# A graph layer with residual and normalisation: VectorE selects the edges of a group four groups ahead throughout, not six

## The chip, the cores and the metric

The kernel runs on one core of a Trainium2 chip. The time is device time in microseconds (us). Engines are called TensorE (PE in the rows, PEld for its weight loads), VectorE (DVE), ScalarE (ACT), GpSimd (POOL) and SyncE (SP).

## What is computed

`x` has 100,000 nodes of 128 features, and there are 50,000 edges (`src`, `dst`) sorted by `dst`. Cut to what matters:

```python
messages = jnp.einsum('ei,oi->eo', x[col], W) + b
out = jax.ops.segment_sum(messages * agg_weight, row, num_segments=x.shape[0])
x = _layernorm(x + out, axis=-1)        # row = src, col = dst
```

So each node receives the projected feature rows of the nodes at the other end of its edges, plus the bias once per edge; that sum is added to the node's own row, and every row is normalised.

## The kernel before

**Two stages.** In the first 270 us or so the 50,000 edges are sorted by receiving node into lists of at most 128 edges; the result is `table`, which holds for each place in a list the row of `x` to gather and the node that receives it. The change doesn't touch that. The second stage walks over 196 groups of 512 nodes (g = 0 to 195; GA is 196). It is written as one stream of instructions for each engine, tied by semaphores that count.

**Lists and periods.** Eight groups make a period (SPAN_G = 8) and have 17 lists. A list belongs to the group in which its window of nodes starts: within a period the groups own 3, 2, 2, 3, 2, 2, 2 and 1 lists. `u` is the group's number modulo 8. The last nodes of a period also fall into the first list of the next period.

**One group, engine by engine.**

- GpSimd gathers the rows of each list into `xg` (L527, 17 gathers a period). It may start on group g once TensorE has summed group g - 8.
- VectorE's `select(g)` splits each gathered fp32 value into three bf16 parts (L984 writes `rest`, L989 writes `xl`) and makes a 0/1 matrix `sel` for each list of the group (L986). It waits for the gathers and for `s_agg`.
- TensorE's `aggregate(g)` multiplies the three parts with `sel` and adds them in PSUM (L707, L709, L711); behind an odd group stand the counts of edges (L721).
- ScalarE's `keep_sums(g)` copies the sum to SBUF as `aggT` (L1094).
- TensorE's `project(g)` multiplies `aggT` with the weights (L737), and adds the bias for an even group and its neighbour (L734).
- VectorE's `add_x(g)` waits for `project(g)` (`s_out`) and adds the loaded `x` (L995, writes `h`); `moments(g)` takes the statistics (L1002); for a pair of groups `invert` and `recentre` follow (L1008, L1013).
- ScalarE's `spread_of` takes the root (L1102), and `normalise` writes `y` in four instructions (L1109). SyncE loads `xt` and stores `y`.

**Order on TensorE.** Round r holds `aggregate(r)` and then `project(r - 2)`: A(6), P(4), A(7), P(5), A(8), P(6) and so on. A(g) is used below for the sums of group g, P(g) for its projection and S(g) for `select(g)`.

**What the sums of a group wait for.** A(g) needs S(g). The last group of a period needs more, since it also uses the first list of the next period. This is the line, in `aggregate`:

```python
pe.wait_ge(s_lower, min(g + 2, GA) if u % SPAN_G == SPAN_G - 1 else g + 1)
```

`s_lower` counts the finished selects, so for u = 7 the sums of group g wait until S(g + 1) is done.

**Order on VectorE.** It is the loop that the change touches. An iteration g holds `add_x(g)`, the selects that `lead` asks for, `moments(g)`, and after every odd group `invert` and `recentre` for the pair. `lead(g)` is how many groups the selects run ahead: 4 for groups 0 to 3, 5 for groups 4 to 7, and 6 from group 8 on. Iteration 3 and iteration 7 therefore hold two selects, and from then on iteration g holds S(g + 6). The buffers `sel`, `rest` and `xl` hold one period (XR = 1), `xg` holds two (RX = 2).

Of the kernel before, what the change touches and what calls it, by code (L numbers as in the profile page):

```python
# [16 lines left out]
def gnn_resnorm_kernel(nc, x, src, dst, W, b, agg_weight, hi_scratch, place_scratch, out, most=128):  # L17
# [56 lines left out]
    with ctx:  # L74
# [6 lines left out]
        def at_least(eng, s, count):  # L81

            if not isinstance(count, int) or count > 0:
                eng.wait_ge(s, count)
# [256 lines left out]
        def rounds(stages):  # L341

            for i in range(GA + max(lag for _, lag in stages)):
                for stage, lag in stages:
                    g = i - lag
                    if 0 <= g < GA:
                        stage(g, g % R, g // R, g // SPAN_G, g // SPAN_G % RX, g // SPAN_G // RX)
# [396 lines left out]
        def _(dve):  # L744
# [163 lines left out]
            def decode(lo, hi):  # L908
                c = slice(lo, hi)
                after(V.tensor_tensor(i2[:, c], i2[:, c], other2[:, c], OR))  # L910
                V.tensor_scalar(emp[:, c], i1[:, c], FULL, FULL, XOR, AND)
                V.tensor_scalar(low4[:, c], i2[:, c], 15 << 25, 25, AND, LSR)
                after(V.tensor_scalar(tabi[:, c], i1[:, c], 8191 << 16, 12, AND, LSR))
                after(V.tensor_tensor(low4[:, c], low4[:, c], tabi[:, c], OR))
                after(V.tensor_scalar(tabi[:, c], emp[:, c], 30, None, LSR))
                after(V.scalar_tensor_tensor(table[:, c, 0], tabi[:, c], part[:], low4[:, c], ALU.mult, ALU.add))
                after(V.tensor_scalar(emp[:, c], emp[:, c], 20, None, LSR))
                after(V.tensor_scalar(tabq[:, c], i2[:, c], (GN - 1) << 16, 16, AND, LSR))
                return V.tensor_tensor(table[:, c, 1], tabq[:, c], emp[:, c], OR)
# [52 lines left out]
            with dve.Else():  # L972
                decode(head, NB).then_inc(s_idx, 1)

                def select(g, u, n, period, m, mn):
                    if g == 0 or g == RX * SPAN_G:
                        dve.wait_ge(s_idx, 1 + period // RX)
                    at_least(dve, s_agg, g - (XR * SPAN_G - 2))
                    mine = [k for k in CLASS[u % SPAN_G] if period * LISTS + k < NB]
                    lists = slice(mine[0], mine[-1] + 1)  # L980
                    if u % SPAN_G == 0:
                        dve.wait_ge(s_first[m], 16 * mn + 16)
                    dve.wait_ge(s_rest[m][u % SPAN_G], 16 * mn * len([k for k in CLASS[u % SPAN_G] if k]) + 16 * len([k for k in mine if k]))
                    V.tensor_tensor(rest[:, m % XR, lists], xg[:, m, lists], top[:, m, lists, :, 1], ALU.subtract).then_inc(s_upper, 1)  # L984
                    for k in mine:
                        V.tensor_scalar(sel[:, m % XR, k, 0:WIDTH[k]], iota_win[:, WIN[k]:WIN[k] + WIDTH[k]],  # L986
                                        table[:, period * LISTS + k, 1:2], None, ALU.is_equal).then_inc(s_sel, 1)
                    dve.wait_ge(s_upper, g + 1)
                    V.tensor_tensor(xl[:, m % XR, lists], rest[:, m % XR, lists], middle[:, m % XR, lists, :, 1], ALU.subtract).then_inc(s_lower, 1)  # L989

                def add_x(g, u, n, period, m, mn):
                    dve.wait_ge(s_out, g + 1)
                    dve.wait_ge(s_x[u], 16 * n + 16)
                    at_least(dve, s_y, 4 * g - 4 * R + 4)
                    V.tensor_tensor(h[:, u].rearrange("p j d -> p (j d)"), OUT[u % RO][:],  # L995
                                    xt[:, u].rearrange("p j d -> p (j d)"), ALU.add).then_inc(s_h, 1)

                def moments(g, u, n, period, m, mn):

                    dve.wait_ge(s_h, g + 1)  # L1000
                    for j in range(0, 4, 2):
                        V.bn_stats(stats[:, u, j:j + 2].rearrange("p two f -> p (two f)"),  # L1002
                                   h[:, u, j:j + 2].rearrange("p two d -> p d two")).then_inc(s_stats, 1)

                def invert(g, u, n, period, m, mn):
                    if u % 2:
                        dve.wait_ge(s_std, g // 2 + 1)
                        V.reciprocal(rstd[:, u - 1:u + 1], std[:, u - 1:u + 1]).then_inc(s_rstd, 1)  # L1008

                def recentre(g, u, n, period, m, mn):  # L1010
                    if u % 2:
                        dve.wait_ge(s_rstd, g // 2 * 2 + 1)
                        V.scalar_tensor_tensor(shift[:, u - 1:u + 1], stats[:, u - 1:u + 1, :, 1], -1.0, rstd[:, u - 1:u + 1],  # L1013
                                               ALU.mult, ALU.mult).then_inc(s_rstd, 1)

                def one(stage, g):
                    if 0 <= g < GA:
                        stage(g, g % R, g // R, g // SPAN_G, g // SPAN_G % RX, g // SPAN_G // RX)

                lead = lambda g: min(6, 4 + g // 4)  # L1020
                for g in range(lead(0)):
                    one(select, g)
                for g in range(GA + 1):
                    one(add_x, g)
                    for ahead in range(g + lead(g), g + 1 + lead(g + 1)):
                        one(select, ahead)
                    one(moments, g)
                    one(invert, g - 1)
                    one(recentre, g - 1)
# [107 lines left out]
```

## Time and profile before

| | us |
|---|---|
| median of 3 runs | 838.07 |
| lowest, highest | 833.6, 838.79 |
| span of the profiled execution | 834.4 |

The span is that of one execution, from its first to its last instruction, and lies inside the range of the three runs. The page does not give time outside the span.

| engine | busy us | share |
|---|---|---|
| VectorE | 769.2 | 92% |
| TensorE matmul | 756.2 | 91% |
| ScalarE | 660.2 | 79% |
| GpSimd | 494.7 | 59% |

These are shares of the whole span. The second stage begins at about 270 us, and from 340 to 800 us it runs evenly; the views of that stretch say more than the page's average. "PEclk" is the TensorE clock granted: 1.00 is 2.4 GHz, 0.5 would be 1.2 GHz.

### The profile page before, as it was taken

What the parts mean: (1) busy time and instruction counts of PE and PEld (TensorE: products, weight loads), DVE (VectorE), ACT (ScalarE), POOL (GpSimd) and SP (SyncE); (2) the same over time, 40 slices, a digit from 0 to 9 for tenths busy, and PEclk for the clock granted to TensorE, in tenths of its full rate; (3) what the DMA queues carried; (4) which work ended last, traced back from release to release, by engine and by line L of the source; (5) the groups of instructions that cost most, each with busy time, mean ns of one, the idle gap of its engine ahead of it and who ended that gap; (6) DMA issues with size and microseconds to landing.
All of it is one profiled execution on the core that took longest, in us unless ns stands there. A gap on an engine that the chain in (4) does not pass through costs nothing.

```text
span 834.4 us, 23648 instructions
## 1 busy us (share of the span) xinstructions
PE 756.2 (91%) x8073; PEld 550.6 (66%) x8073; DVE 769.2 (92%) x2547; ACT 660.2 (79%) x1659; POOL 494.7 (59%) x510
## 2 busy tenths in 40 slices
PE   4889999999999978999998899999999999899894
PEld 3844555555554656777777777777777777677773
DVE  7989999999998788999999999998999999999995
ACT  2157878787885368899888889888889888888898
POOL 2024333333421777777777777777777777777750
PEclk9999999999999999999999999999999999999998
DMA  2001110111113257888777788777777878778773
GB/s 78 2 27 40 28 40 28 32 36 28 41 35 103 61 177 223 246 243 254 235 253 232 238 241 247 246 237 235 233 248 245 254 234 248 228 251 252 232 240 135
DMA packets 78148, 139.46 MB, mean 167 GB/s; under 512 B 16864, under 2 KB 17900, under 8 KB 78028
## 3 DMA queue, kind: packets, MB, share of 16 engines
q1 hardware_dynamic: 62476, 110.50, 39.5%
q0 software_dynamic: 15552, 27.43, 14.4%
q8 instruction: 66, 1.08, 0.5%
q14 instruction: 54, 0.44, 0.2%
HBM read 86.04 MB, written 51.83 MB: 165 GB/s over the span
## 4 chain that ended last, share of the span: by engine, by line
PE 37%; DVE 27%; issue 13%; DMA 8%; POOL 7%; ACT 7%; ACTq 0%; POOLq 0%; SPq 0%; DVEq 0%
PE bank L737 10%; DMA xg<-in_x,table 8%; POOL xg L527 7%; PE bank L660 5%; DVE stats L1002 4%; DVE oh_s L891 4%; DVE sel L986 3%; ACT y L1109 3%; PE bank L707 3%; PE bank L711 3%; PE bank L709 3%; DVE oh_t L893 3%; DVE rest L984 3%; DVE xl L989 2%; PE bank L553 2%
## 5 line engine op out<-in xcount | busy, mean ns | idle before, releaser
L527 POOL DMA_INDIRECT xg<-in_x,table x417 | 415.7, 997 | 147.5 <-issue 100.3
L1109 ACT ACTIVATE y<-h,shift,rstd 128x128 f32<-128x128 f32 x784 | 321.6, 482 | 24.5 <-DVE shift L1013 24.4
L737 PE MATMUL bank<-wT,aggT 128*128 128x128 f32 x1568 | 229.0, 290 | 0.0
L737 PEld LDWEIGHTS bank<-wT,aggT 128*128 128x128 f32 x1568 | 191.6, 193 | 27.4 <-issue 10.8
L709 PE MATMUL bank<-sel,rest 128*128 128x385 bf16 (+25 forms) x708 | 183.7, 261 | 0.0
L707 PE MATMUL bank<-sel,xg 128*128 128x385 bf16 (+25 forms) x708 | 176.6, 262 | 3.2 <-DVE xl L989 3.0
L711 PE MATMUL bank<-sel,xl 128*128 128x385 bf16 (+25 forms) x708 | 174.9, 261 | 0.0
L479 POOL DMA_INDIRECT place_scratch<-word_col,place_row x69 | 71.6, 1038 | 131.3 <-DVE place_row L882 108.0
L1002 DVE BATCH_NORM_STATS2 stats<-h 128x6 f32<-128x256 f32 x392 | 148.0, 418 | 0.2
L995 DVE TENSOR_TENSOR h<-bank,xt 128x512 f32<-128x512 f32 x196 | 133.7, 682 | 5.9 <-PE bank L737 5.1
L660 PE MATMUL bank<-oh_t,oh_s 128*128 128x417 bf16 x644 | 129.0, 345 | 6.2 <-ACT oh_s L1073 0.8
L1094 ACT COPY aggT<-bank 128x512 f32<-128x512 f32 x196 | 110.8, 565 | 20.2 <-PE bank L711 20.1
L986 DVE TENSOR_SCALAR sel<-iota_win,table 128x385 bf16<-128x385 f16 (+1 forms) x417 | 121.0, 336 | 0.0
L891 DVE TENSOR_SCALAR oh_s<-iota_nb,slot,word_col 128x128 bf16<-128x128 f16 x322 | 107.3, 333 | 0.6 <-PE bank L660 0.4
L984 DVE TENSOR_TENSOR rest<-xg 128x384 f32<-128x384 f32 (+1 forms) x196 | 85.1, 434 | 23.5 <-DMA xg<-in_x,table 22.8
L893 DVE TENSOR_SCALAR oh_t<-iota_nb,t_now 128x417 bf16<-128x417 f16 x322 | 106.0, 329 | 0.0
L1073 ACT ACTIVATE oh_s<-oh_s,ratio_col 128x128 bf16<-128x128 bf16 x322 | 102.8, 393 | 3.3 <-DVE oh_s L891 2.2
L660 PEld LDWEIGHTS bank<-oh_t,oh_s 128*128 128x128 bf16 x644 | 58.0, 98 | 57.3 <-DVE oh_t L893 14.1
L989 DVE TENSOR_TENSOR xl<-rest 128x384 bf16<-128x384 f32 (+1 forms) x196 | 84.5, 431 | 0.0
L707 PEld LDWEIGHTS bank<-sel,xg 128*128 128x128 bf16 x708 | 69.8, 99 | 19.7 <-DVE xl L989 3.4
L709 PEld LDWEIGHTS bank<-sel,rest 128*128 128x128 bf16 x708 | 69.0, 98 | 18.0 <-issue 0.5
L711 PEld LDWEIGHTS bank<-sel,xl 128*128 128x128 bf16 x708 | 69.0, 98 | 16.0 <-issue 0.5
(156 smaller groups left out, 743.1 us busy)
## 6 DMA issues: line engine op xcount, KB each, us to landing
xt<-in_x SPq DMA_DIRECT2D x195, 256.0 KB
out<-y SPq DMA_DIRECT2D x195, 256.0 KB
xg<-in_x,table POOLq DMA_INDIRECT x417
hi_row<-hi_scratch SPq DMA_DIRECT2D x50, 128.0 KB
place_scratch<-word_col,place_row POOLq DMA_INDIRECT x69
place_scratch<-scattered SPq DMA_DIRECT2D x1, 417.0 KB, 3.5
scattered<-place_scratch SPq DMA_DIRECT2D x1, 417.0 KB, 3.2
src_rows<-in_src SPq DMA_DIRECT2D x1, 192.0 KB
```

Source lines behind the costliest of these rows:

```text
L527: nc.gpsimd.indirect_dma_start(out=xg[:, m, k], out_offset=None, in_=x, in_offset=bass.IndirectOffsetOnAxis(ap=table[:, period * LISTS + k ...
L660: last = nc.tensor.matmul(TABLES[w][:, 0:NB], hot, oh_t[:, no % RING], start=(no == 0), stop=False, skip_group_check=True)
L707: nc.tensor.matmul(AGG[q][:, nodes], top[:, ring, k, :, 1], sel[:, half, k, cols], start=(i == 0), stop=False, skip_group_check=True)
L709: nc.tensor.matmul(AGG[q][:, nodes], middle[:, half, k, :, 1], sel[:, half, k, cols], start=False, stop=False, skip_group_check=True)
L711: last = nc.tensor.matmul(AGG[q][:, nodes], xl[:, half, k], sel[:, half, k, cols], start=False, stop=(i == len(lists) - 1), skip_group_che ...
L737: last = nc.tensor.matmul(OUT[u % RO][:, nodes[j]], aggT[:, u % RO, nodes[j]], wT[:], start=False, stop=True, skip_group_check=True)
L891: V.tensor_scalar(oh_s1[:, no % RING], iota_nb[:, 0:P], slot[:, q, i:i + 1], w1_col[:, k * BC + i:k * BC + i + 1], ALU.is_equal, ALU.mult) ...
L893: V.tensor_scalar(oh_t[:, no % RING], iota_nb[:], t_now[:, q, i:i + 1], None, ALU.is_equal).then_inc(s_oh, 1)
L986: V.tensor_scalar(sel[:, m % XR, k, 0:WIDTH[k]], iota_win[:, WIN[k]:WIN[k] + WIDTH[k]], table[:, period * LISTS + k, 1:2], None, ALU.is_eq ...
L995: V.tensor_tensor(h[:, u].rearrange("p j d -> p (j d)"), OUT[u % RO][:], xt[:, u].rearrange("p j d -> p (j d)"), ALU.add).then_inc(s_h, 1)
L1002: V.bn_stats(stats[:, u, j:j + 2].rearrange("p two f -> p (two f)"), h[:, u, j:j + 2].rearrange("p two d -> p d two")).then_inc(s_stats, 1)
L1109: nc.scalar.activation(y[:, u, j], h[:, u, j], ACT.Identity, bias=shift[:, u, j:j + 1], scale=rstd[:, u, j:j + 1]).then_inc(s_y, 1)
```

## The change

```diff
-                lead = lambda g: min(6, 4 + g // 4)
+                lead = lambda g: 4
                 for g in range(lead(0)):
                     one(select, g)
                 for g in range(GA + 1):
```

Every iteration g now holds S(g + 4) and nothing else of the selects. No instruction is added or removed, and no other engine's order changes.

The first place is VectorE's order around the first select of a period, in the evenly running part. The row with `s_first0` is the start of that select, S(8k), and `s_x2` marks `add_x` of a group with u = 2, `s_x4` one with u = 4. Before:

```order
L995 TENSOR_TENSOR h<-bank6,xt 128x512 [waits s_y,s_x2,s_out]
L984 TENSOR_TENSOR rest<-xg 128x384 [waits s_rest0_0,s_first0,s_agg]
L986 TENSOR_SCALAR sel<-iota_win,table 128x385 x3
L989 TENSOR_TENSOR xl<-rest 128x384 [waits s_upper]
L1002 BN_STATS stats<-h 128x6 [waits s_h]
L1002 BN_STATS stats<-h 128x6
L1008 RECIPROCAL rstd<-std 128x8 [waits s_std]
L1013 SCALAR_TENSOR_TENSOR shift<-stats,rstd 128x8 [waits s_rstd]
L995 TENSOR_TENSOR h<-bank7,xt 128x512 [waits s_y,s_x3,s_out]
```

After:

```order
L995 TENSOR_TENSOR h<-bank2,xt 128x512 [waits s_y,s_x4,s_out]
L984 TENSOR_TENSOR rest<-xg 128x384 [waits s_rest0_0,s_first0,s_agg]
L986 TENSOR_SCALAR sel<-iota_win,table 128x385 x3
L989 TENSOR_TENSOR xl<-rest 128x384 [waits s_upper]
L1002 BN_STATS stats<-h 128x6 [waits s_h]
L1002 BN_STATS stats<-h 128x6
L1008 RECIPROCAL rstd<-std 128x8 [waits s_std]
L1013 SCALAR_TENSOR_TENSOR shift<-stats,rstd 128x8 [waits s_rstd]
L995 TENSOR_TENSOR h<-bank3,xt 128x512 [waits s_y,s_x5,s_out]
```

The same select of three lists has moved behind `add_x` of the group two later: S(8) stands behind the addition of group 4 where the even part of before has it behind that of group 2 of the same period.

The second place is the start of TensorE's sums of a group, the same in both kernels. The first row's wait on `s_lower` is the one that the last group of a period makes for the next period's first select:

```order
L737 MATMUL bank<-wT,aggT 128x128 x4
L707 MATMUL bank<-sel,xg 128x151 [waits s_aggc,s_sel,s_lower]
L709 MATMUL bank<-sel,rest 128x151
L711 MATMUL bank<-sel,xl 128x151
L707 MATMUL bank<-sel,xg 128x385
```

Here nothing moved: the projection (L737) stands ahead of these sums, so a late select holds back the sums and every projection behind them.

## Rows read from the trace of the kernel before

**Rows 1.** Windows view: busy us and count of each engine; granted clock; DMA.

```profile
core 0: us, PE busy (x) PEld busy (x) DVE busy (x) ACT busy (x) POOL busy (x), PEclk, DMA share, GB/s
377.00:798.00 421.00, 392.74 (x4039) 313.16 (x4036) 404.87 (x1237) 369.11 (x913) 322.58 (x323) 1.00 0.78 242
```

**Rows 2.** View of line L995 (`add_x`), groups 32 to 184: count, duration, first and last start.

```profile
L995 DVE TENSOR_TENSOR h<-bank,xt x153: 661/691/693, 377.6 to 798.1; 128x512 f32<-128x512 f32 x153
```

**Rows 3.** Waits of VectorE, 377 to 799 us: total us, times, longest.

```profile
DVE rest L984 <- DMA xg<-in_x,table: 11.4, 17, 1.4
DVE h L995 <- PE bank L737: 1.0, 2, 0.5
DVE h L995 <- issue: 0.6, 2, 0.3
```

**Rows 4.** Waits of TensorE in the same stretch.

```profile
PE bank L734 <- ACT aggT L1094: 26.2, 27, 2.1
```

**Rows 5.** Timeline, VectorE: start us, us; from add_x(98) to add_x(99).

```profile
559.31 0.67 DVE L995 TENSOR_TENSOR h<-bank,xt 128x512 f32<-128x512 f32 x1
...
561.05 0.55 DVE L989 TENSOR_TENSOR xl<-rest 128x384 bf16<-128x384 f32 x1
...
562.52 0.69 DVE L995 TENSOR_TENSOR h<-bank,xt 128x512 f32<-128x512 f32 x1
```

**Rows 6.** Timeline, TensorE: P(100), start of A(103), P(101), start of A(104).

```profile
563.13 1.16 PE L737 MATMUL bank<-wT,aggT 128*128 128x128 f32 x8
...
564.12 0.18 PE L707 MATMUL bank<-sel,xg 128*128 128x31 bf16 x1
...
565.79 1.16 PE L737 MATMUL bank<-wT,aggT 128*128 128x128 f32 x8
...
566.78 0.27 PE L707 MATMUL bank<-sel,xg 128*128 128x241 bf16 x1
```

**Rows 7.** Timeline, TensorE: P(4), start of A(7), P(5).

```profile
291.61 1.16 PE L737 MATMUL bank<-wT,aggT 128*128 128x128 f32 x8
...
295.21 0.19 PE L707 MATMUL bank<-sel,xg 128*128 128x31 bf16 x1 [2.44 <-DVE xl L989]
...
298.00 1.60 PE L737 MATMUL bank<-wT,aggT 128*128 128x128 f32 x8
```

**Rows 8.** Timeline, VectorE: last part of S(8), and add_x(5).

```profile
294.61 0.55 DVE L989 TENSOR_TENSOR xl<-rest 128x384 bf16<-128x384 f32 x1
...
299.64 0.69 DVE L995 TENSOR_TENSOR h<-bank,xt 128x512 f32<-128x512 f32 x1 [0.92 <-PE bank L737]
```

**Rows 9.** Timeline, TensorE: the other four pauses of over 1.8 us.

```profile
313.35 0.40 PE L734 MATMUL bank<-b,deg 32*128 32x128 bf16 x8 [2.56 <-ACT aggT L1094]
...
325.89 0.40 PE L734 MATMUL bank<-b,deg 32*128 32x128 bf16 x8 [1.87 <-ACT aggT L1094]
...
575.03 0.40 PE L734 MATMUL bank<-b,deg 32*128 32x128 bf16 x8 [1.97 <-ACT aggT L1094]
...
729.80 0.40 PE L734 MATMUL bank<-b,deg 32*128 32x128 bf16 x8 [2.12 <-ACT aggT L1094]
```

**Rows 10.** Windows view behind each of the five pauses.

```profile
295.00:299.00 4.00, 3.79 (x25) 2.52 (x26) 3.58 (x12) 3.08 (x8) 3.08 (x4) 0.57 0.38 117
...
312.00:316.00 4.00, 2.65 (x32) 2.25 (x34) 3.61 (x12) 4.00 (x11) 3.09 (x4) 1.00 0.62 176
...
326.00:330.00 4.00, 4.00 (x27) 3.07 (x25) 4.00 (x13) 3.19 (x9) 3.08 (x4) 0.57 0.85 229
575.00:579.00 4.00, 3.97 (x25) 3.23 (x26) 3.90 (x12) 3.68 (x10) 3.05 (x3) 0.57 0.84 234
...
729.00:733.00 4.00, 3.19 (x37) 2.66 (x38) 3.97 (x13) 3.68 (x10) 2.92 (x4) 1.00 0.75 202
```

**Rows 11.** Timeline, VectorE: add_x of groups 192, 193 and 194.

```profile
819.05 0.69 DVE L995 TENSOR_TENSOR h<-bank,xt 128x512 f32<-128x512 f32 x1 [1.33 <-PE bank L737]
...
821.62 0.69 DVE L995 TENSOR_TENSOR h<-bank,xt 128x512 f32<-128x512 f32 x1 [0.78 <-PE bank L737]
...
823.76 0.69 DVE L995 TENSOR_TENSOR h<-bank,xt 128x512 f32<-128x512 f32 x1 [0.66 <-PE bank L737]
```

**Rows 12.** Groups view, 377 to 798 us: gathers; busy us, mean ns; idle before.

```profile
L527 POOL DMA_INDIRECT xg<-in_x,table x323 | 322.9, 1000 | 98.4 <-issue 77.4 <-PE bank L737 11.6 <-PE bank L711 9.4
```

## The prediction

> **What bounds the kernel now.** I read the windows view first, because the page's average mixes the sorting with the groups. In the even part VectorE is busy for 404.87 of 421 us, 96%; TensorE shows 393, ScalarE 369, and GpSimd 323 [rows 1]. The reader should see three engines close together with VectorE first. The 152 steps from group 32 to group 184 take 798.1 - 377.6 = 420.5 us [rows 2], so a group costs 2.77 us and a period of eight 22.1 us. The gathers are close to that too: 323 of them, with 322.9 us busy and 98.4 us between them, fill the whole stretch, 17 x 1.30 = 22.2 us a period [rows 12].
>
> The waits come second. VectorE loses 11.4 us in 17 waits for gathered rows, and only 1.0 us in two waits for a projection, with 0.6 us of issue [rows 3]: 13.0 us in 19 periods, 0.68 us a period. The work of VectorE that nothing interrupts is therefore 22.1 - 0.7 = 21.4 us a period. TensorE waits 26.2 us for ScalarE's copy of the sums [rows 4]; that costs nothing now, because VectorE comes to a finished projection later than it ends. TensorE never waits for a select in this stretch.
>
> The timeline comes third, for how much room a select has. S(104) ends at 561.05 + 0.55 = 561.60 us [rows 5]. A(103), the last group of its period, needs that select and starts at 564.12, 2.5 us later; A(104) starts at 566.78, 5.2 us later [rows 6]. A round of TensorE is 566.78 - 564.12 = 2.66 us.
>
> **The change, step by step.**
>
> 1. Instructions. None is added or removed. Each select runs two iterations later, 2 x 2.77 = 5.5 us at today's pace. An ordinary group's room of 5.2 us comes out at about zero; the room of 2.5 us of a period's last group comes out at -3 us. So the ordinary groups are just in time, and once a period TensorE must stop.
>
> 2. The stop itself, by the order of the program. Let (4), (5), (7), (8) stand for the groups at these places. A(7) needs S(8). S(8) now stands behind `add_x(4)`, which needs P(4), and P(4) is the last thing that TensorE does before A(7). So TensorE can't have run ahead: it stops from P(4) until VectorE has added and selected three lists. In today's rows that takes from 559.31 to 561.60, 2.29 us [rows 5]. With the handovers about 2.4 us of TensorE pause, in each period. For TensorE alone this is harmless: eight rounds of 2.6 us are 21 us.
>
> 3. What is late next: VectorE. After S(8) it has only the moments, reciprocal and shift, 562.52 - 561.60 = 0.92 us [rows 5]. Then `add_x(5)` waits for P(5), which stands behind A(7). From the start of A(7) to the end of P(5) the same pair took 564.12 to 565.79 + 1.16 = 566.95, 2.83 us [rows 6]. With 0.06 and 0.04 us of handover VectorE waits 2.83 + 0.10 - 0.92 = 2.0 us. Behind it stand S(9) and everything else, so it adds to the chain. Later in the period VectorE works 2.4 to 3.2 us an iteration against TensorE's 2.66 us a round, and I find only about 0.1 us of further waits.
>
> 4. What is given back: the gathers. A select that runs 5.5 us later relative to the gathers finds them landed, so I take the 0.68 us of waits a period away [rows 3]. With a longer period GpSimd's 22.2 us [rows 12] no longer bind. Net for the stop: 2.0 + 0.1 - 0.7 = 1.4 us a period.
>
> 5. ScalarE. Its copies now meet a VectorE that is in step with TensorE, so part of the 26.2 us, 1.4 us a period [rows 4], may be exposed. Nothing to all of it are the bounds; following one period I find the copy late by 0.2 to 0.4 us in one round, and take 0.2 us.
>
> 6. The clock. The kernel before already has one such stop, in the ramp: S(8) ends at 295.16 [rows 8] and A(7) starts at 295.21 after an idle 2.44 us [rows 7]. The granted clock over 295 to 299 us is 0.57, so the 1.2 GHz level for most of it [rows 10]. A(7) to the end of P(5) takes 299.60 - 295.21 = 4.39 us instead of 2.83, and `add_x(5)` waits for it [rows 7, 8]. A fall costs 1.56 us. How often? There are five pauses of TensorE over 1.8 us: 2.44 [rows 7], and 2.56, 1.87, 1.97 and 2.12 [rows 9]. Behind three the clock falls, behind two (2.56 and 2.12, the longest and the third) it stays at 1.00 [rows 10]. Of the three pauses over 2 us it is one. Between one in three and three in five I take 45%, 10 of 23 stops: 16 us. The bounds are none and all: 0 and 36 us.
>
> The Trainium skill's page "TensorE: Matmul & The Clock Gate", section "HAM oscillation — how this bites in real kernels", describes a pause that recurs with each tile of a loop and says that the cold start is then paid on each tile. By that rule the term would be 23 x 1.56 = 36 us instead of 16. The rows agree only in part: two of five pauses of this length left the clock alone.
>
> 7. How many. Groups 15, 23, ... 191 give 23 stops; that of group 7 is there today. At the end only four groups instead of six are left without a select, in which VectorE waits for TensorE, 2.8 us in all today [rows 11]. I give 2 us back.
>
> **The sum.** 23 x (1.4 + 0.2) = 37 us, minus 2, plus 16, is 51 us on the span of 834.4: 885 us. The page shows no time outside the span, and the median run is 3.7 us above it, which is within the spread of the three; I add 1 us: 886.
>
> **The rivals.**
>
> - *The clock stays up* in all stops. For it: two of five pauses, and a longer one than mine among them. Against it: the stop of group 7, the very same pair of steps, did bring it down. 834.4 + 35 = 869; with nothing for ScalarE 865. Chance 14%.
> - *The clock falls in every stop*, the rule above. 834.4 + 35 + 36 = 905. Chance 8%.
> - *Faster.* VectorE's waits for gathers decide, and the stop is hidden. Then the waits go (0.68 x 23 = 16 us) and 2 us at the end: 817. The place is `add_x(5)`: the sign turns where A(7) and P(5) take less than 0.92 + 0.68 = 1.6 us after S(8). They took 2.83 [rows 6], and the order of the two engines leaves no way around it. Chance 2%.
> - *No measurable change*, within about 8 us: the stop costs VectorE 2.0 us but the slack returns more than the named waits, because the small gaps between VectorE's instructions (421 - 404.87 - 13.0 = 3.1 us) or the speed of selects beside fewer gathers count too. That takes 0.16 off a period for the gaps; to reach +8 us the stop would have to be under 0.4 us a period. Chance 4%.
> - *The change does nothing*, because `lead` isn't used so: excluded, the order shows each select moved.
>
> **How the numbers follow.** The forecast, stops in every period with the clock down in some, has 72%. Its own range goes from 860 (the lowest stop: 2.0 - 0.68 - 0.16 = 1.16 us, 27 us, minus 2.8, plus two falls at 3 us) to 908 (all falls and 0.3 us of ScalarE, with the rounding of my handovers). It takes in the first two rivals nearly whole, so I leave the range there. Slower by over 1%, which is about what a measurement can tell from no change, has 94%; within 1% 4%; faster 2%.
>
> **What would show it.** In the profile after: idle time of L707 put down to DVE L989, of some 2.4 us once in each period, at every start of A with u = 7; waits of VectorE's L995 on L737, about 23 of 2 us or 3.5 us, 50 to 65 us in total; waits for gathered rows near nothing; add_x of groups 32 to 184 further apart, 24.4 us a period instead of 22.1; the granted clock of the even part between 0.93 and 0.97. If L995 waits in every group and not once a period, step 3 is wrong, and then TensorE or ScalarE is in step at each group and the time is above my range. If L995's waits are right and the clock stays 1.00, only step 6 is wrong. If waits for gathers remain, step 4 is.

## The result, and the profile after

| | before | after |
|---|---|---|
| median, us (6 runs each) | 837.03 | 893.31 |
| lowest, highest | 833.6, 838.79 | 880.83, 901.13 |
| span of the profiled execution | 834.4 | 897.0 |

The ratio is 1.056, with a 95% interval of 1.053 to 1.059: the change makes the kernel 5.6% slower, about 47 us. The runs after lie in a band of 20 us. The ratio leaves out the three longest of them (898.73 to 901.13 us), of which the profiled execution is one; between the medians of all six runs lie 56 us, 6.7%. So the profile shows every kind of loss, and more of one of them than the ratio holds.

The windows view of the same stretch as [rows 1], kernel after; the columns are busy us and count of each engine, the granted clock and DMA:

```profile
377.00:798.00 421.00, 374.15 (x3597) 288.14 (x3594) 364.23 (x1105) 332.33 (x812) 289.22 (x288) 0.94 0.69 216
```

VectorE is busy for 364 of 421 us where it was busy for 405, and TensorE's granted clock is 0.94 where it was 1.00. The view of `add_x` over groups 32 to 184 answers to [rows 2]:

```profile
L995 DVE TENSOR_TENSOR h<-bank,xt x153: 662/691/693, 385.9 to 857.7; 128x512 f32<-128x512 f32 x153
```

19 periods take 471.8 us instead of 420.5, so 24.8 us each instead of 22.1. The waits of VectorE and of TensorE from 377 to 799 us (total us, times, longest) answer to [rows 3] and [rows 4]; these are all that are left. The stretch is as long as there, but holds only 17 of the stops:

```profile
DVE h L995 <- PE bank L737: 56.0, 22, 4.2
```

```profile
PE bank L707 <- DVE xl L989: 46.7, 33, 2.5
```

The waits for gathered rows, 11.4 us before, are gone, and so is TensorE's wait of 26.2 us for ScalarE. In their place VectorE waits 56 us for projections and TensorE 47 us for selects. This is one stop in TensorE's timeline, P(100) and P(101) around the start of A(103), in the places of [rows 6]:

```profile
597.22 1.16 PE L737 MATMUL bank<-wT,aggT 128*128 128x128 f32 x8
...
600.83 0.19 PE L707 MATMUL bank<-sel,xg 128*128 128x31 bf16 x1 [2.45 <-DVE xl L989]
...
602.51 1.16 PE L737 MATMUL bank<-wT,aggT 128*128 128x128 f32 x8
```

And VectorE's timeline at the same stop: `add_x(100)`, the last part of S(104), the shift, and `add_x(101)`:

```profile
598.49 0.67 DVE L995 TENSOR_TENSOR h<-bank,xt 128x512 f32<-128x512 f32 x1
...
600.23 0.55 DVE L989 TENSOR_TENSOR xl<-rest 128x384 bf16<-128x384 f32 x1
...
601.59 0.17 DVE L1013 SCALAR_TENSOR_TENSOR shift<-stats,rstd 128x8 f32<-128x8 f32 x1
603.71 0.69 DVE L995 TENSOR_TENSOR h<-bank,xt 128x512 f32<-128x512 f32 x1 [1.96 <-PE bank L737]
```

Read the two together. TensorE ends P(100) at 598.38 and is idle for 2.45 us, until S(104) is done at 600.78 (597.22 + 1.16, and 600.23 + 0.55). VectorE is then out of work at 601.76 and idle until P(101) ends at 603.67. The two engines take turns in standing still.

The two stops before it show the second kind of loss. `add_x` in VectorE's timeline there, kernel after, to be held against the wait of 1.96 us above:

```profile
554.55 0.69 DVE L995 TENSOR_TENSOR h<-bank,xt 128x512 f32<-128x512 f32 x1 [4.19 <-PE bank L737]
557.53 0.69 DVE L995 TENSOR_TENSOR h<-bank,xt 128x512 f32<-128x512 f32 x1 [0.48 <-PE bank L737]
...
580.10 0.69 DVE L995 TENSOR_TENSOR h<-bank,xt 128x512 f32<-128x512 f32 x1 [3.51 <-PE bank L737]
```

The pause of TensorE was 2.4 us in all three. The waits of VectorE differ, and the windows behind the three starts of A (549.44, 575.67 and 600.83) say why (column PEclk):

```profile
549.00:553.00 4.00, 3.56 (x22) 2.15 (x23) 1.33 (x5) 1.03 (x2) 1.76 (x3) 0.50 0.75 245
553.00:555.00 2.00, 2.00 (x12) 1.78 (x11) 0.45 (x1) 1.68 (x5) 0.42 (x1) 0.50 0.11 33
576.00:579.00 3.00, 3.00 (x19) 1.74 (x17) 0.56 (x3) 0.96 (x2) 0.46 (x1) 0.50 0.73 249
580.00:582.00 2.00, 2.00 (x23) 1.53 (x22) 1.90 (x6) 1.34 (x3) 1.11 (x1) 1.00 0.31 104
601.00:605.00 4.00, 4.00 (x46) 2.93 (x42) 2.01 (x8) 2.85 (x7) 2.19 (x3) 1.00 0.68 227
```

At 0.50 the granted clock is at the 1.2 GHz level. At the first stop it is still there from 553 to 555 us, past the end of the late projection, and the next projection is late too (the 0.48 us); at the second it is back at 1.00 when the late projection has ended; at the third it doesn't fall. Of the 23 stops from group 15 on, seven have a wait of 1.95 to 1.96 us (no fall), nine one of 3.2 to 3.5 us, and seven one of 4.2 us, each of these with a further 0.5 us at the addition after it. With 1.4 us for a stop (the filled kernel below gives it) and 1.5 or 2.7 us for a fall (3.51 - 1.96, and 4.19 + 0.5 - 1.96), the 62.6 us between the spans are about accounted for: stops 23 x 1.4 = 32, falls 9 x 1.5 + 7 x 2.7 = 32, and some 2 us less at the end.

### The profile page after: what moved, and what is told of

It is laid out like the page before. It is cut to its first block, busy times and chain, and to the rows that moved or that the text cites. A ratio compares the mean times of both kernels' runs of the same rounds, so it can differ in the third digit from the quotient of the medians.

```text
span 897.0 us, 23648 instructions
## 1 busy us (share of the span) xinstructions
PE 791.9 (88%) x8073; PEld 564.5 (63%) x8073; DVE 770.0 (86%) x2547; ACT 665.9 (74%) x1659; POOL 497.5 (55%) x510
## 4 chain that ended last, share of the span: by engine, by line
DVE 44%; PE 40%; issue 11%; ACT 3%; DMA 1%; ACTq 0%; POOL 0%; SPq 0%; DVEq 0%; POOLq 0%
PE bank L737 10%; DVE sel L986 8%; DVE stats L1002 8%; DVE rest L984 7%; PE bank L660 6%; DVE xl L989 6%; PE bank L707 4%; PE bank L709 4%; PE bank L711 4%; DVE oh_s L891 3%; DVE h L995 3%; PE bank L721 3%; DVE oh_t L893 3%; PE bank L553 2%; ACT same_hi L1053 2%
## 5 line engine op out<-in xcount | busy, mean ns | idle before, releaser
L707 PE MATMUL bank<-sel,xg 128*128 128x385 bf16 (+25 forms) x708 | 184.6, 274 | 66.0 <-DVE xl L989 65.9
L737 PE MATMUL bank<-wT,aggT 128*128 128x128 f32 x1568 | 236.9, 296 | 0.0
L737 PEld LDWEIGHTS bank<-wT,aggT 128*128 128x128 f32 x1568 | 199.1, 199 | 30.1 <-issue 7.3
L995 DVE TENSOR_TENSOR h<-bank,xt 128x512 f32<-128x512 f32 x196 | 134.2, 685 | 83.9 <-PE bank L737 83.0
L709 PE MATMUL bank<-sel,rest 128*128 128x385 bf16 (+25 forms) x708 | 191.7, 272 | 0.0
L711 PE MATMUL bank<-sel,xl 128*128 128x385 bf16 (+25 forms) x708 | 182.7, 271 | 0.0
L709 PEld LDWEIGHTS bank<-sel,rest 128*128 128x128 bf16 x708 | 71.2, 102 | 20.0 <-issue 2.9
L711 PEld LDWEIGHTS bank<-sel,xl 128*128 128x128 bf16 x708 | 71.8, 101 | 19.1 <-issue 4.1
```

Source lines behind the costliest of these rows:

```text
L707: nc.tensor.matmul(AGG[q][:, nodes], top[:, ring, k, :, 1], sel[:, half, k, cols], start=(i == 0), stop=False, skip_group_check=True)
L709: nc.tensor.matmul(AGG[q][:, nodes], middle[:, half, k, :, 1], sel[:, half, k, cols], start=False, stop=False, skip_group_check=True)
L711: last = nc.tensor.matmul(AGG[q][:, nodes], xl[:, half, k], sel[:, half, k, cols], start=False, stop=(i == len(lists) - 1), skip_group_che ...
L737: last = nc.tensor.matmul(OUT[u % RO][:, nodes[j]], aggT[:, u % RO, nodes[j]], wT[:], start=False, stop=True, skip_group_check=True)
```

## The experiments

All are variants of the changed kernel unless said otherwise, each compared with the kernel before on the same chip in the same session (835.2 to 835.6 us there).

**The clock alone.** TensorE gets nine matmuls to do in the stop, whose result is overwritten later. They wait until `add_x(4)` is done, and so stand between P(4) and the wait for S(8):

```diff
+                    if u % SPAN_G == SPAN_G - 1:
+                        pe.wait_ge(s_h, g - 3)
+                        for _ in range(9):
+                            nc.tensor.matmul(OUT[u % RO][:], ident_bf[:], age_col[:].rearrange("p c e -> p (c e)"),
+                                             start=True, stop=True, skip_group_check=True)
                     pe.wait_ge(s_lower, min(g + 2, GA) if u % SPAN_G == SPAN_G - 1 else g + 1)
```

> The changed kernel, with nine extra matmuls of 128x512 on TensorE (their result is overwritten later) between P(4) and the wait for S(8), in each of the 24 stops. They take about 1.9 of the 2.4 us pause. Theory A (a stop costs 1.4 us a period by VectorE's wait for P(5), and the rest of the loss is the clock's falls): the granted clock of the even part is 1.00, VectorE's waits for a projection are about 2.0 us, 23 times, and the time is that of before plus 33 to 37 us, 869 to 874 us. Theory B (the clock's falls follow from something else than the pause, or cost nothing): the clock still falls and the time stays at 880 to 900 us.

Measured 864.0 us, ratio 1.036 (1.032 to 1.039). The windows view over all stops, and a stop's `add_x` (L1000 here), in its profile:

```profile
296.00:830.00 534.00, 516.05 (x5017) 390.15 (x5038) 484.95 (x1479) 444.96 (x1093) 395.90 (x394) 1.00 0.75 229
```

```profile
602.41 0.69 DVE L1000 TENSOR_TENSOR h<-bank,xt 128x512 f32<-128x512 f32 x1 [1.95 <-PE bank L742]
```

The clock never falls, and VectorE still waits 1.95 us. So the stops with the clock up cost 3.6% of 835.6, 30 us, which is less than the 33 to 37 expected. What the changed kernel has beyond this is the clock's. By the ratios it is 1.056 - 1.036, 17 us; but that ratio leaves out the runs after with the most falls. By the medians of all runs it is 56 - 28 = 28 us.

**The changed kernel again**, in the second session.

> The changed kernel once more, beside the next ones on the same chip, for the number of falls of the clock. Theory A: 24 stops of 2.4 us, always at the same place; periods come in steps: 23.6 us without a fall of the clock, about 25.0 and 26.3 us with one, and which stops have one differs from execution to execution, so the times spread over 880 to 900 us. Theory B (the falls hang on something in the data or the lists): the same stops have a fall as in the first profile.

Measured 890.0 us (887.08 to 904.94), ratio 1.065 (1.062 to 1.068). The stop of A(39), as `add_x(37)`, in this profile and in the first one:

```profile
400.42 0.69 DVE L995 TENSOR_TENSOR h<-bank,xt 128x512 f32<-128x512 f32 x1 [1.96 <-PE bank L737]
```

```profile
402.60 0.69 DVE L995 TENSOR_TENSOR h<-bank,xt 128x512 f32<-128x512 f32 x1 [3.52 <-PE bank L737]
```

The same stop with the same data has no fall here and had one there; the periods of this profile are again about 23.6, 25.0 and 26.3 us, and 17 of its 23 stops have a fall. So the stop belongs to the program, and whether it has a fall does not. The falls make the band of 20 us between executions: in the first six runs the mean granted clock is 0.975 and 0.969 in the two of 881 and 882 us, 0.952 in the one of 888, and 0.939 to 0.949 in the three of 899 to 901. Against the filled stop the second session's ratio is 1.065 - 1.036, 24 us, and by the medians of all runs the difference is 55 - 28, some 26 us.

**One select moved back by one iteration.** S(8k) joins S(8k - 1) in the iteration ahead:

```diff
-                lead = lambda g: 4
+                lead = lambda g: 5 if g % 8 == 4 else 4
```

> The changed kernel, but iteration 3 of every period does both S(7) and S(8), iteration 4 none: all selects stand four groups ahead except the first of a period, which stands five ahead. Theory A: one select moved by one iteration takes the whole loss away; 834 to 845 us, the clock at 1.00, A(7) waits at most a few tenths of a us more than an ordinary group. Theory B (lead four leaves the ordinary groups without room too, and they cost a share): 850 us or more.

Measured 831.8 us (median of 11 runs), ratio 0.996 (0.993 to 0.999). One select in eight, one iteration earlier, takes the whole loss away; ordinary groups at lead four cost nothing. That the time is below the expected range's bottom I had not foreseen. Eight of the 11 runs took 829.7 to 834.0 us and three 841.1 to 845.8. The profile is of one of the three (844.12 us, span 841.5). It shows that in that execution the stop hasn't gone but shrunk:

```profile
568.02 0.19 PE L707 MATMUL bank<-sel,xg 128*128 128x31 bf16 x1 [1.40 <-DVE xl L989]
```

```profile
570.89 0.69 DVE L995 TENSOR_TENSOR h<-bank,xt 128x512 f32<-128x512 f32 x1 [0.57 <-PE bank L737]
```

"A few tenths of a us" was wrong for TensorE (1.40 us of pause). VectorE waits 0.57 us a period, and with the other waits 12.9 us in 19 periods, where the kernel before has 13.0 [rows 3]. Yet these 19 periods take 430.2 us instead of 420.5: in this execution the selects themselves took longer, as the last section says. No short execution was profiled, so its waits are not shown.

**The projection ahead of the sums.** The stop stays, but P(5) no longer stands behind A(7):

```diff
-                rounds([(aggregate, 0), (project, 2)])
+                for r in range(GA + 2):
+                    pair = [(aggregate, r), (project, r - 2)]
+                    for stage, g in pair[::-1] if r % SPAN_G == SPAN_G - 1 else pair:
+                        at(stage, g)
```

> The changed kernel, but on TensorE P(5) stands ahead of A(7) in the last round of each period, so that it runs inside the stop. The stop itself stays. Theory A (the pause of TensorE costs nothing by itself, VectorE's wait for P(5) behind A(7) is the price): VectorE's waits for a projection nearly vanish, TensorE's pause for the select shrinks to about 1.2 us, and the time is 834 to 845 us. Theory B (the pause of TensorE itself is lost): 860 us or more.

Measured 844.5 us, ratio 1.010 (1.007 to 1.013). The two waits views of the even part:

```profile
DVE h L1002 <- PE bank L737: 16.5, 18, 1.0
```

```profile
PE bank L707 <- DVE xl L996: 35.8, 37, 1.6
```

TensorE's pause is 1.56 us instead of the 1.2 expected, still there once a period, and four fifths of the loss are gone. The part that I had expected to vanish, VectorE's wait, has halved (0.91 us in most periods) and moved:

```profile
391.75 0.69 DVE L1002 TENSOR_TENSOR h<-bank,xt 128x512 f32<-128x512 f32 x1
...
395.23 0.69 DVE L1002 TENSOR_TENSOR h<-bank,xt 128x512 f32<-128x512 f32 x1 [0.99 <-PE bank L737]
```

The addition of group 37 (u = 5) at 391.75 starts at once; that of group 38 (u = 6) waits 0.99 us, because P(6) stands behind both A(7) and A(8). A wait taken away at one projection comes back, smaller, at the next.

**The wait ahead of the last list.** Only the last list of A(7) needs S(8), so the wait moves there (the wait on the count of `sel` matrices, left out below, is split in the same way):

```diff
-                    pe.wait_ge(s_lower, min(g + 2, GA) if u % SPAN_G == SPAN_G - 1 else g + 1)
+                    pe.wait_ge(s_lower, g + 1)
...
                     for i, (ring, half, k, cols, nodes) in enumerate(lists):
+                        if u % SPAN_G == SPAN_G - 1 and i == len(lists) - 1:
+                            pe.wait_ge(s_lower, min(g + 2, GA))
```

> The changed kernel, but A(7) waits for S(8) only ahead of its last list, the only one that needs it; the first three lists' sums, 0.91 us of TensorE, run before. Theory A (the price is VectorE's wait for what TensorE has to do between S(8) and the end of P(5)): that wait falls from 2.0 to 1.1 us a period, 23 x 0.9 = 21 us less, and the pause of TensorE falls to 1.5 us, at which no fall of the clock was seen: 843 us, 838 to 850. Theory B (the price is the late select, whatever TensorE does first): 860 us or more.

Measured 845.4 us, ratio 1.012 (1.010 to 1.015). A stop in its profile (L996 is `add_x`):

```profile
594.06 0.69 DVE L996 TENSOR_TENSOR h<-bank,xt 128x512 f32<-128x512 f32 x1 [1.04 <-PE bank L738]
```

The wait is 1.04 us, as the 0.91 us of TensorE's work moved ahead of the stop would have it, and the select is as late as in the changed kernel. So the lateness of the select has no price of its own; its price is what TensorE has yet to do for VectorE when it arrives. The 10 us that are left agree: 23 x (1.04 - 0.68) = 8 us, and at one stop the clock fell (2.48 and 1.34 us of wait). Against the filled stop (845 and 864 us) the gain is VectorE's wait, since the clock fell at none of the stops there.

**Five groups ahead**, twice, in two sessions:

```diff
-                lead = lambda g: 4
+                lead = lambda g: 4 + (g > 3)
```

> The selects run five groups ahead from group 4 on, between before (six) and the change (four). Theory A (the price hangs on one dependence, that of the last group of a period on the first select of the next): S(8) then stands in iteration 3, ahead of the addition of group 4, so no stop; the room of A(7) falls from 2.5 us to about zero. Time within 1% of before, 832 to 842 us, the waits for gathers (11.4 us) smaller. Theory B (each group of lead costs its share, because VectorE and TensorE come into step): about half of the loss, 855 to 865 us.

> Five groups ahead once more. If the gain of 0.4% over before was real, the ratio is again 0.994 to 0.998; if it was chance of one chip and session, it is 1.000.

Measured 832.3 and 832.6 us, ratios 0.996 (0.994 to 0.998) and 0.997 (0.995 to 0.998). The loss doesn't come in proportion to the lead: six to five gains 3 us, five to four loses 50 to 57 by the ratios. VectorE's waits at five (first session):

```profile
DVE rest L984 <- DMA xg<-in_x,table: 8.0, 10, 3.3
```

They are 8.0 us for gathered rows (9.0 in the second session) where six groups ahead have 11.4 [rows 3].

**Around five.** Two more versions looked for what five leaves, and one for the other side of six. Five with the first select of a period at six is `lambda g: 4 + (g > 3) + (g > 3 and g % 8 == 3)`:

> Five groups ahead and the first select of each period six. If what is left of waits at five groups is A(7)'s (5.7 us in the even part) it goes away: 829 to 832 us, a little below five groups alone (832.3). If the gathers decide instead, the time is 832 to 835 us and the waits for gathered rows are above 8.0 us in the even part.

Measured 838.8 us, ratio 1.005 (1.003 to 1.006), slower than either expectation's range:

```profile
DVE rest L984 <- DMA xg<-in_x,table: 12.5, 11, 2.1
PE bank L707 <- DVE xl L989: 1.8, 3, 0.8
```

TensorE's waits for selects fell (1.8 from 5.7 us) and VectorE's for gathers rose to 12.5 us, as the second reading had it. But the waits don't account for the time: with those for projections VectorE waits 13.9 us here, and 10.5 and 13.1 us in the two profiles of five groups alone, which are 6 us faster. What the rest is stays open. Five with the late wait:

> Five groups ahead, and the wait of a period's last group for the next period's first select stands ahead of its last list only. At five groups TensorE still waits 5.7 us for selects in the even part, but VectorE hardly waits for projections (1.3 us), so by the theory that only VectorE's waits cost, there is little to gain: 830 to 833 us, no more than 1.5 us from five groups alone. A gain of 3 us or more would say that TensorE's own waits cost too.

Measured 832.9 us, ratio 0.997 (0.995 to 0.999): no gain over five alone. TensorE's own waits for selects cost nothing here. Seven groups, `lambda g: min(7, 4 + g // 4)`:

> Seven groups ahead instead of six from group 12 on. Theory: VectorE then meets the gathers earlier; its waits for gathered rows rise from 11.4 us in the even part to 20 us or more and the time is 838 to 850 us. If the gathers' waits stay at 11 us and the time within 0.3% of before, the lead has no price on its long side.

Measured 838.7 us, ratio 1.004 (1.003 to 1.006). The time is as expected and the reason is not: the waits for gathers in the even part are lower than before, 8.9 us, not 20.

```profile
L995 DVE TENSOR_TENSOR h<-bank,xt x153: 661/690/693, 380.2 to 801.6; 128x512 f32<-128x512 f32 x153
```

Group 32 is added at 380.2 us instead of 377.6, but VectorE has by then done one select more, which takes 1.6 us on average; 421.4 us for the 19 periods behind it are nearly the 420.5 of before. In the ramp from 297 to 377 us the waits for gathers are 5.8 us where they were 3.3, but over the whole second stage VectorE waits no longer than before (27.2 and 26.0 us, of that for gathers 18.6 and 19.8). So what the 3 us are is not shown.

## Why the prediction was right, and where not

The forecast was 886 us, the median is 893.3; the mechanism was right, and one term of the sum, the clock's, was sized too low. That 886 us against 838 gives almost the ratio that was measured, 1.057 against 1.056, is in part luck: the ratio holds the three shortest runs after, and by the medians of all runs the change costs 56 us and not the 48 forecast. (The low end of its range, 834.4 + 27 - 2.8 + 3, is 861 or 862 and not 860, which changes nothing.)

1. *The stop (steps 1 and 2)*, 2.3 us of select and about 2.4 us of pause, once in each period at u = 7: the pause is 2.40 to 2.46 us at each of the 24. The ordinary groups are just in time, as step 1 had it: about one other group a period waits, for some 0.3 us, and moving the boundary's select alone brought everything back.

2. *VectorE's wait (step 3)*, 2.0 us by adding A(7), P(5) and handovers and taking off 0.92: it measured 1.95 to 1.96 us wherever the clock stayed up. The late wait shifted it by what the step says, 0.9 us.

3. *What is given back (step 4)*, 0.68 us a period: right. Of these 0.68 us only 0.60 are waits for gathers (11.4 us in 19 periods), the rest are the other waits of [rows 3]; none of them is left in the even part. Step 3's further 0.1 us of waits did not show where the clock stayed up. The whole of a stop, put at 1.4 us, measures 1.4 us in the filled kernel (446.7 us for its 19 periods against 420.5, of which 37.1 - 13.0 = 24.1 us are waits of VectorE), and 1.5 us in the changed kernel between two stops without a fall (A starts at 600.83 and 624.45 us, 23.6 against 22.1).

4. *ScalarE (step 5)*, 0.2 us a period, was wrong: it is nothing. TensorE has no wait for `aggT` left in the even part, and the filled stop lost 28 to 30 us where the sum without the clock had 35. Why the copy is never late is not shown.

5. *The clock (step 6)*, 10 falls of 1.56 us, 16 us, is the term that was too low. It fits only the runs that the first ratio holds (17 us over the filled stop); the second session's ratio gives 24 us, the medians of all runs 26 to 28, and the profile 32. Both factors were low. The price of a fall, 1.56 us, was that of one kind: seven of the 16 falls in the profile cost 2.7 us, since the 1.2 GHz level outlasted A(7) and P(5), and a second projection was late too. And 16 and 17 of 23 stops had a fall in the two profiles, not 10; both profiles are of long executions. So VectorE's waits for projections from group 13 on add up to 78 us in the profile, above the 50 to 65 us that were to show it. The errors of steps 5 and 6, +5 and -8 to -16, partly cancel.

The page "TensorE: Matmul & The Clock Gate" of the Trainium skill, section "HAM oscillation — how this bites in real kernels", whose cold start at each tile was a rival, describes a kernel that waits some 3 to 5 us each time; the pauses here are shorter. They bear the rule out in part: 16 of 23 stops in one profile had a fall, while seven pauses of the same length, 2.40 to 2.46 us, had none.

6. *The count and the end (step 7)*: the waits of VectorE for the last projections went from 2.8 us to 1.3, so 1.5 us came back, not 2. The stop of group 7 was not quite "there today". In the kernel before S(8) stands behind `add_x(3)`, and it is late because it waits for its gathered rows:

```profile
293.40 0.56 DVE L984 TENSOR_TENSOR rest<-xg 128x384 f32<-128x384 f32 x1 [1.48 <-DMA xg<-in_x,table]
```

VectorE then has S(9) to do as well and waits 0.92 us for P(5) [rows 8]; in the kernel after it has not, and waits 3.51 us. TensorE's pause is the same, 2.44 and 2.43 us, so the price of a fall could be read from it.

The rival of a faster kernel had its turning point at 1.6 us between S(8) and the end of P(5). One version bears this out and one is undecided. With the late wait VectorE waits 1.04 us a period, above 0.68, and the time is 1.2% over. With the first select early the wait is 0.57 us, below 0.68, and the median is below that of before; but the 0.57 us were read in an execution that was itself longer than before.

## What to carry to other kernels

When a producer's lead is cut, look first for the one consumer that needs more than its own item, here the last group of a period, which needs the next period's first select; the room of the ordinary groups (5.2 us) says nothing about it. Where the two engines depend on each other in a loop, a stop of one is paid by the other: add what the stopped engine still has to do for the waiting one, and subtract what that one has left to work on. A pause of TensorE can cost again as much through its clock, and if a pause can't be avoided, independent matmuls in it can keep the clock up: they saved 17 to 24 us of 47 to 54 here by the ratios, and 26 to 28 of 55 to 56 by the medians of all runs.

## What was not expected of the hardware

The same program with the same data took from 881 to 905 us, in steps that can be counted: periods of 23.6, 25.0 or 26.3 us, as TensorE's clock stayed at 2.4 GHz after a pause of 2.4 us, or went to 1.2 GHz for a shorter or a longer time. With the pauses filled, four runs lay within 5 us (862.6 to 867.7).

The length of a pause alone doesn't decide whether the clock falls. With seven groups ahead a pause of 3.00 us left it at 1.00, and with five and the first select at six one of 1.46 us was followed by a fall. TensorE's timeline at each, and the window behind it, first seven groups ahead, then the other:

```profile
327.40 0.40 PE L734 MATMUL bank<-b,deg 32*128 32x128 bf16 x8 [3.00 <-ACT aggT L1094]
327.00:331.00 4.00, 3.60 (x37) 2.91 (x38) 3.72 (x12) 3.21 (x9) 3.08 (x4) 1.00 0.73 218
```

```profile
391.54 0.50 PE L734 MATMUL bank<-b,deg 32*128 32x128 bf16 x8 [1.46 <-ACT aggT L1094]
391.00:395.00 4.00, 3.46 (x21) 2.83 (x22) 3.25 (x9) 4.00 (x11) 3.08 (x3) 0.59 0.76 225
```

What else decides is not shown.

In two profiles whose periods repeat to 0.1 us, with one or two exceptions (first select early, projection first), VectorE's selects `sel` took longer on average, 358 and 350 ns against 334 ns in the groups view of the kernel before, with the same median of 319 ns in all three; so a few of them take longer. With the first select early that is 323 x 24 ns = 8 of the 10 us by which the profiled 19 periods exceed those of before. With the late wait the periods vary between 22.4 and 22.8 us, and `sel` takes 341 ns. So it may be that a kernel locked to its own period meets the same collision each time, but nothing here tests it, and what would collide stays open.
